# Layer 1's weight splits after the first image, a projection behind the first scores, and a transpose ahead of a restack

## The reference

```python
# layer 0
Bm, Cm, Dm = Wb @ x, Wc @ x, Wd @ x              # (C, n)
S = softmax(Bm.T @ Cm)                            # (n, n)
y = gamma * (Dm @ S.T) + x
# layer 1
hn = group_norm(y)                                # 32 groups
q, k, v = wq @ hn + bq, wk @ hn + bk, wv @ hn + bv    # 4 heads of 64
out = softmax(q.T @ k / 8) @ v                    # per head
result = y + wp @ out + bp
```

## Time and profile before

| | us |
|---|---|
| median of 3 runs | 682.79 (682.38 to 683.4) |
| the profiled execution | 682.95 |
| its span, first to last instruction | 681.0 |
| TensorE busy | 668.9 |
| VectorE busy | 560.4 |
| ScalarE busy | 455.7 |
| GpSimd busy | 231.2 |

### The profile page before, as it was taken

How to read it: one execution, slowest core, us unless ns; L and a number is a source line. 1 busy time by engine, 2 the same in 40 slices (tenths; PEclk the granted TensorE clock), 3 DMA queues, 4 the chain that set the end, 5 groups by cost and what they waited for, 6 DMA issues and landing times.

```text
span 681.0 us, 11125 instructions
## 1 busy us (share of the span) xinstructions
PE 668.9 (98%) x3668; PEld 568.5 (83%) x3668; DVE 560.4 (82%) x910; ACT 455.7 (67%) x790; POOL 231.2 (34%) x216
## 2 busy tenths in 40 slices
PE   8989999999999899999999999999999999999997
PEld 7878888888888778888888888888888888988886
DVE  4787768768678478998888899888899888889996
ACT  5563435435435167988787788777789778778884
POOL 0130211201125024565233465242546433334531
PEclk9999999999999999999999999999999999999999
DMA  7476856645645957001656010367110265301001
GB/s 227 85 134 188 170 99 138 155 100 128 165 97 123 213 141 203 1 1 48 146 119 185 17 47 1 93 155 193 54 54 8 58 157 126 92 16 47 1 32 62
DMA packets 96714, 69.50 MB, mean 102 GB/s; under 512 B 71072, under 2 KB 73376, under 8 KB 96672
## 3 DMA queue, kind: packets, MB, share of 16 engines
q1 hardware_dynamic: 96672, 68.97, 41.8%
HBM read 18.62 MB, written 8.39 MB: 40 GB/s over the span
## 4 chain that ended last, share of the span: by engine, by line
PE 86%; DVE 5%; issue 3%; ACT 2%; POOL 2%; DMA 1%; SPq 1%; POOLq 0%; DVEq 0%; ACTq 0%
PE acc L1410 36%; PE scores L1410 26%; PE trans L1444 16%; PE trans L1410 8%; DVE negmax L979 1%; ACT prob L739 1%; DMA x_raw<-in_x 1%; POOL planes L638 1%; DVE pt_lo L997 1%; ACT pt_hi L749 1%; DVE pt_lo L1168 1%; DMA turned<-planes 0%; POOL y_in L649 0%; SPq L466 0%; DVE qk L1132 0%
## 5 line engine op out<-in xcount | busy, mean ns | idle before, releaser
L626 POOL TENSOR_SCALAR prob<-prob,rsum 128x1024 f32<-128x1024 f32 x127 | 142.8, 1124 | 256.7 <-DVE rsum L984 256.7
L739 ACT ACTIVATE prob<-scores,negmax 128x1024 f32<-128x1024 f32 x160 | 178.9, 1118 | 74.4 <-DVE negmax L979 72.9
L979 DVE TENSOR_REDUCE negmax<-scores 128x1 f32<-128x1024 f32 x160 | 194.0, 1213 | 17.8 <-PE scores L1410 16.6
L749 ACT ACTIVATE pt_hi<-trans 128x512 fp32r<-128x512 f32 x256 | 139.6, 594 | 63.9 <-PE trans L1444 63.3
L997 DVE TENSOR_TENSOR pt_lo<-trans,pt_hi 128x512 fp32r<-128x512 f32 x256 | 163.5, 680 | 1.0 <-ACT pt_hi L749 0.6
L1410 PE MATMUL scores<-k_st,q_st 128*128 128x512 f32 x512 | 137.9, 391 | 0.7 <-issue 0.7
L1444 PEld LDWEIGHTS trans<-ident,prob 128*128 128x128 f32 x1024 | 117.7, 140 | 22.5 <-issue 4.2
L1444 PE MATMUL trans<-ident,prob 128*128 128x128 f32 x1024 | 134.6, 273 | 1.2 <-DVE pt_lo L997 1.1
L1410 PEld LDWEIGHTS scores<-k_st,q_st 128*128 128x128 f32 x512 | 95.7, 188 | 21.6 <-issue 1.2
L1410 PE MATMUL acc<-pt_hi,v_st 128*128 128x512 f32 (+1 forms) x264 | 106.8, 407 | 0.6 <-DVE pt_lo L997 0.6
L1410 PE MATMUL acc<-pt_lo,v_st 128*128 128x512 f32 (+1 forms) x264 | 101.0, 385 | 0.0
(11 more groups left out here) (163 smaller groups left out, 1028.0 us busy)
## 6 DMA issues: line engine op xcount, KB each, us to landing
k_st<-qk SPq DMA_DIRECT2D x64, 256.0 KB, 4.7
q_st<-qk SPq DMA_DIRECT2D x64, 128.0 KB, 2.4
x_raw<-in_x SPq DMA_DIRECT2D x8, 512.0 KB, 5.2
y_out<-in_x SPq DMA_DIRECT2D x16, 256.0 KB, 3.3
y_scratch<-y_out SPq DMA_DIRECT2D x16, 256.0 KB, 2.3
y_in<-y_scratch SPq DMA_DIRECT2D x4, 1024.0 KB, 7.5
y_res<-y_scratch SPq DMA_DIRECT2D x16, 256.0 KB, 3.7
out<-y_res SPq DMA_DIRECT2D x14, 256.0 KB, 2.1
```

The source lines that it names most:

```text
L626: nc.gpsimd.tensor_scalar(p, p, rsum[:, t % 2:t % 2 + 1], 1.0, ALU.mult, ALU.mult)\
L739: nc.scalar.activation(prob[:, t % 2, :], scores[:, t % 2, :], ACT.Exp, bias=negmax[:, t % 2:t % 2 + 1], scale=1.0, accum_out=rowsum[:, t ...
L749: nc.scalar.activation(pt_block(pt_hi, (t // 4) % 2, t, h), trans[:, h, :].rearrange("p (j n) -> p j n", n=P), ACT.Copy).then_inc(pt_high, 1)
L979: nc.vector.tensor_reduce(negmax[:, t % 2:t % 2 + 1], scores[:, t % 2, :], AX_X, ALU.max, negate=True).then_inc(max_ready, 1)
```

## The change

Four edits. (1) The later weights other than d are split in the first image's tail: on ScalarE and VectorE behind turned tile 7; `bq8` goes with them, and TensorE's wait for them moves from `d0` to `next_qk0` of the last image. (2) `w_later` moves in memory from under `pt_hi` to under `h_hi`, which is written in the last image. (3) The group `a3` of the first image goes behind `scores0(0, 0)` on TensorE, behind the first exponential on ScalarE and behind the first reciprocal on VectorE. (4) On SyncE the last image's turn 7 goes ahead of restack `next_qk0`.

```diff
-LEAD_IN = [("a0", None), ("a1", None), (None, "d"), ("a2", "q"), ("a3", "k"), (None, "v"), (None, "p")]
+LEAD_IN = [("a0", None), ("a1", None), (None, "d"), ("a2", None)]
...
-        w_later = sb("w_later", [P, len(LATER_WEIGHTS), KT, C], F32, start)
-        w_raw.update({w: w_later[:, n, :, :] for n, w in enumerate(LATER_WEIGHTS)})
...
         prob = sb("prob", [P, 2, N])
+        until_split = ExitStack()
+        w_later = sb("w_later", [P, len(LATER_WEIGHTS), KT, C], F32, until_split)
+        until_split.close()
+        w_raw.update({w: w_later[:, n, :, :] for n, w in enumerate(LATER_WEIGHTS)})
         h_hi = sb("h_hi", [P, KT, N], F32R)
...
             turn(IMAGES - 1, 6)
+            turn(IMAGES - 1, 7)
             restack(last_plan, "next_qk0")
-            turn(IMAGES - 1, 7)
...
             for s in range(T0_IMAGE):
                 exp0(0, s)
+                if s == 0:
+                    a_high(plan_first_a, "a3")
...
             turned_high(0, 7)
+            for w in LATER_WEIGHTS[1:]:
+                weight_high(w)
...
-            dve.wait_ge(vec_loaded, 16)
-            nc.vector.tensor_scalar(bq8[:, :], vec[:, BQ:BQ + 2], QSCALE, None, ALU.mult).then_inc(w_split, 1)
...
                 recip(0, t)
+                if t == 0:
+                    a_low(plan_first_a, "a3", HIGH0)
...
             for t in range(T0_IMAGE - TURN_LAG, T0_IMAGE):
                 turned_low(0, t)
+            for w in LATER_WEIGHTS[1:]:
+                weight_low(w)
+            dve.wait_ge(vec_loaded, 16)
+            nc.vector.tensor_scalar(bq8[:, :], vec[:, BQ:BQ + 2], QSCALE, None, ALU.mult).then_inc(w_split, 1)
...
-            for n, name in enumerate(FIRST_A):
+            def first_a(n):
+
+                name = FIRST_A[n]
...
+            for n in range(3):
+                first_a(n)
...
                 scores0(0, s)
+                if s == 0:
+                    first_a(3)
                 if s in D_STEPS:
                     if s == D_STEPS[0]:
-                        pe.wait_ge(w_split, len(WEIGHTS) + 1)
+                        pe.wait_ge(w_split, WEIGHTS.index("d") + 1)
...
             scores0(e, 7)
+            pe.wait_ge(w_split, len(WEIGHTS) + 1)
             pe.wait_ge(h_split, 4)
             chunk(last_plan, "next_qk0")
```

## The result

The changed kernel takes 686.65 us (median of 6, 685.64 to 687.05) against 683.09 for the kernel before beside it: ratio 1.0051, 95% interval 1.0038 to 1.0064, slower by 3.5 us. The profiled execution took 687.05, its span is 685.3 against 681.0.

The account below looks back on a forecast made before the run. TensorE, busy 98% of the span, was taken as the bound, through its fixed work and stands. Losses 0.37 + 1.83 + 0.39 = 2.59 us on the median 682.79 gave 685.4 us, range 683.0 to 686.8.

Parts of the forecast that it names:

- rival C: Last image: transposes hold up the restacks, whose copies land late; part 3 then costs 1.2 to 1.8, run 686.5; chance 0.13.
- Part 2: First image's tail: the four splits delay the first result and image 1's first scores; two new TensorE stands, 1.83 us lost.
- Part 1: Start: with `a3` moved behind them, first scores wait for `a1`'s low part; 0.37 us lost, freed VectorE time gains nothing.
- the 1.77 us: TensorE's stand before the first image's first value product; forecast to stay, despite the earlier first maximum.
- The 2.48 put in front: VectorE, first image's tail: four splits and `bq8` add 2.48 us ahead of the first result and later low parts.
- Part 3: Last image: moving the turn delays restack `qk0`, so ScalarE writes `qk2` later; TensorE's stand becomes 2.5 us, 0.39 lost.
- Rival A: Last image: slot wait ends before the turn, so the early turn gains 1.7 us; run 683.3, chance 0.13.
- the prediction's rule on completion order: Last image's DMA: a completion lands only after earlier writes of its engine; transposes landing at 225.5 delay nothing beyond 227.67.

Follow-up runs that it names:

- this part alone: Kernel before with group `a3` behind the first scores on all three engines, splits kept in the lead-in: 683.46 us, ratio 0.9999.
- the dose raised: Kernel before with groups `a2` and `a3` both behind the first scores, splits kept in the lead-in: 684.81 us against 683.53, ratio 1.0020.
- step5_first: Kernel before with VectorE's low parts of d3 and turned tile 3 ahead of tile 5's low plane in the first image's step 5: 682.83 against 684.00 us.
- turn_first_only: Kernel before with only the last image's turn 7 moved ahead of restack `next_qk0` on SyncE: 683.60 us against 683.57, ratio 1.0001.
- splits_in_tail_only: Kernel before with only edits 1 and 2 (splits in the tail, `w_later` under `h_hi`); `a3` and the turn as before: 685.87 us, ratio 1.0038.
- changed_turn_back: Changed kernel with the SyncE swap undone, restack `next_qk0` again ahead of turn 7: 685.69 us, ratio 1.0037 to the kernel before.
- three_stands: Kernel before with `step5_first`, `qk2_ahead`, the tail's first result ahead of turned tile 7's low part, two stores behind the restacks: 679.93 against 684.00 us.
- qk2_ahead: Kernel before with `qk2` split ahead of turned tile 7 on ScalarE and VectorE in the last image, SyncE's order kept: 683.27 against 684.00 us.

## Why the prediction was right, and where it was off

The side and all three mechanisms held. The size was a quarter too small: 2.6 us forecast, 3.5 measured. The 686.65 lies just inside the range, 0.15 below its upper end, outside the 684.7 to 686.0 of the forecast itself and nearest to rival C's 686.5. C's mechanism did not occur; the range reached that far because of it, so there is some luck in the hit. What made up the difference is part 2 and the clock.

- **Part 1**, 0.37 forecast. The trace has 0.36 between `a1`'s low part and the first value product, and 0.34 with this part alone. Alone it is not seen in the times; with the dose raised it is, at 1.3 to 1.4 for a forecast 1.7. That the 1.77 us stay was right, and `step5_first` shows why: they are VectorE's own order behind the fourth maximum.
- **Part 2**, 1.83 forecast. It is the term that was mis-sized: 2.17 alone and 2.30 in the changed kernel, each with 0.1 of restart. The 2.48 put in front were exact (58.17 to 60.65). The missing part is the start of the tail: turned tile 7 reached ScalarE 9.80 us behind the first value product in the trace of before and 10.0 to 10.6 behind it in the nine others that have the old order in step 5, five of which leave the tail as it was (10.0 to 10.6 too). So nothing marks it as an effect of the change, and the trace of before was the earliest of ten. Of the 0.57 that are missing (2.30 against 1.73 without the restart) 0.49 is this landing. I took one execution's landing as fixed. Before, 0.75 us of slack (61.07 to 61.93, less the release) hid the spread; with VectorE's tail made the longest chain, it became time. The idle rows ahead of the low part of tile 7 say it, 1.21 us before and 1.75 after.
- **Part 3**, 0.39 forecast. The stand grew by 0.49 in the changed kernel, 0.43 in `turn_first_only`, for the forecast reason. Less the shift of 3.04, the turned tile reached ScalarE at 224.03 (forecast 224.1) and the restack released it at 227.81 (forecast 227.67). Rival A is out: the restack's landing comes after the turn, not before 226.2. Of rival C, the copies landing late, nothing shows: the median of `q_st` from issue to landing was 2.5 (219 to 254 us) against 2.4, and the prediction's rule on completion order had nothing to decide, as the second turned plane was in use at 228.56 and the restack released ScalarE at 230.85.
- **Left out**: the clock. It added 0.75 net in the profiled run. The granted clock was below 1.000 in all six runs of the changed kernel and in about half of those before, so a part of this is in the 3.5 us as well. A part of the profiled 4.33 (0.24 at the start) is no effect of the change. The medians differ by 3.56: the profiled run of the changed kernel was the slowest of its six, 0.40 above their median, and that of before 0.14 below its own.

Sum from the profile: 0.24 + 0.36 + 2.30 + 0.14 (the restarts; 3.04 is the shift of the last matmul ahead of `av2`'s stand) + 0.49 + 0.75 = 4.28 of 4.33.

What stays open: whether part 3 alone costs its 0.4 at the end. The trace of `turn_first_only` has 0.45 from the first value product to the last product, but layer 1 alone differs by 0.3 between traces of the same code. The spans gave 0.1, and those of the runs below full clock speak against a whole 0.4. With a store more in front, the loss is clear.

## What to carry to other kernels

Work moved off a busy start is free only where the new place has idle time in front of the next release. The same four splits cost 2.3 us at one place of the tail and nothing in the idle stretches a few us ahead of it and behind it. Before a transfer is put ahead of another in one queue, look who reuses the buffer of the one that is passed: that wait takes the removed one's place. And of a slack read from one profile, keep the spread of the DMA that ends it.

## What the runs showed of the hardware

In about half of the runs of the kernel before (32 of 71) the mean granted clock was 0.997 instead of 1.000. In the three traces that have it, none of them of the kernel before, it is one stretch of some 3.4 us at half clock (1.2 instead of 2.4 GHz) that begins 0.4 to 0.6 us behind the end of a stand of TensorE (2.60 us in the changed kernel, 2.12 in `splits_in_tail_only`, 1.84 in `changed_turn_back`). In the runs of the kernel before that have it the span is longer by 0.5 us on average (681.62 against 681.14; 0.6, 0.6 and 0.1 in the three series of runs). How often it comes goes roughly with the stand ahead of `av2`: 0 of 5 runs with 1.35 us (`three_stands`), 1 of 11 with 1.38 (`qk2_ahead`), 32 of 71 with 2.11 (and 24 of 45 in the four kernels that left it at 2.1 or 2.2 and added no other of its size), 7 of 11 with 2.54, 6 of 6 in the changed kernel with 2.60, 10 of 11 with 3.06. Taken together that is 1 of 16 below 1.4 us, 56 of 116 at 2.1 to 2.2, and 23 of 28 above 2.5; the 7 of 11 at 2.54 do not stand out by themselves, and the changed kernel has the new stand of 1.57 besides. It is also seen behind another stand, of 1.84 us in `changed_turn_back` (3 of 5 runs); `splits_in_tail_only`, with 2.12 and 1.45, had it in 1 of 5. So a stand of 2 us can have a price beyond its length, in some runs and not in others of the same program. The Trainium skill (TensorE: Matmul & The Clock Gate, Part 1: The HAM clock gate) describes these two clock levels and a gate whose own rhythm is not tied to the kernel's start. The counts agree with that: the kernel is the same in each run, and the fall comes in some runs only. That this rhythm is the reason is not shown here.
